# State space stage: rows of B and C spread a turn ahead, output projection in two halves

## The reference

```python
xz = x @ Win + bin                      # x is layernormed
xs, z = jnp.split(xz, 2, axis=-1)       # 256 inner channels each
xs = silu(xs)
xp = xs @ Wx + bx                       # dp (8), Bs (16), Cs (16)
delta = softplus(dp @ Wdt + bdt)
A = -jnp.exp(A_log)                     # 256 channels x 16 states
# for each token t, from h = 0:
h = exp(delta_t[:, None] * A) * h + (delta_t * xs_t)[:, None] * B_t[None, :]
hidden_t = h @ C_t
y = (hidden + xs * Dp) * silu(z)
x = x + y @ Wout + bout
```

## Time and profile before

| | |
|---|---|
| time, median of 3 runs | 6864.2 us (6859.29 to 6873.38) |
| the profiled execution | 6861.8 us, its span 6859.7 us |
| state space stage within it | about 1980 to 2684 us |
| busy over the whole span | PE 6081.4 us (89%), DVE 4362.3 (64%), ACT 3526.7 (51%), POOL 2191.8 (32%) |
| granted TensorE clock | mean 0.94 of full speed |

### The profile page before, as it was taken

One profiled execution on the slowest core, in us unless ns is written; L12 is line 12 of the kernel. 1 busy time (PEld: TensorE's weight loads), 2 busy tenths in 40 slices (PEclk: granted clock), 3 DMA queues, 4 the chain that ended last, 5 costly groups with the idle time before them and its releaser, 6 DMA issues. The chain is left out here.

```text
span 6859.7 us, 128543 instructions
## 1 busy us (share of the span) xinstructions
PE 6081.4 (89%) x50945; PEld 3477.3 (51%) x50945; DVE 4362.3 (64%) x7548; ACT 3526.7 (51%) x5768; POOL 2191.8 (32%) x1461
## 2 busy tenths in 40 slices
PE   7999987999877777998658999999999999999998
PEld 4666664444432223676434555555555555555554
DVE  3444443444348886333447888888888888888885
ACT  3434433666434443443425666666666666666664
POOL 0000000222214443000005555555555555555553
PEclk9999987999968888999769999999999999999999
DMA  1000000222200000000001111111111111111111
GB/s 52 1 1 1 1 1 13 50 50 49 61 8 0 0 1 0 1 0 0 0 22 35 32 41 41 32 38 42 35 37 43 36 34 45 36 32 46 39 37 26
DMA packets 183558, 174.97 MB, mean 26 GB/s; under 512 B 24021, under 2 KB 174070, under 8 KB 182774
## 3 DMA queue, kind: packets, MB, share of 16 engines
q1 hardware_dynamic: 182998, 167.18, 10.2%
HBM read 30.79 MB, written 2.10 MB: 5 GB/s over the span
## 5 line engine op out<-in xcount | busy, mean ns | idle before, releaser
L2367 POOL TENSOR_TENSOR local_ssum<-local_sq 128x512 f32<-128x512 f32 x384 | 696.3, 1813 | 2298.0 <-ACT local_sq L2155 2297.8
L2375 POOL TENSOR_TENSOR local_rot<-local_rot,local_inv_all 128x512 f32<-128x512 f32 x768 | 964.3, 1287 | 92.8 <-DMA local_inv_all<-local_inv 92.5
L1976 PE MATMUL banks<-local_y,local_Wqkv 128*128 128x512 f32 x1536 | 824.5, 619 | 63.9 <-ACT local_sq L2155 61.0
L861 POOL TENSOR_TENSOR cosine_summed<-cosine_probs 128x512 f32<-128x512 f32 x128 | 172.6, 1349 | 1678.6 <-ACT cosine_probs L750 1678.5
L2177 ACT ACTIVATE local_probs<-local_probs,local_npeak 128x1152 f32<-128x1152 f32 x384 | 482.7, 1257 | 355.2 <-DVE local_probs L2281 355.2
L2281 DVE TENSOR_TENSOR local_probs<-banks,band 128x576 f32<-128x576 f32 x768 | 546.2, 753 | 184.2 <-PE banks L2011 178.9
L2261 DVE TENSOR_TENSOR local_rot<-banks,local_rotary_scaled 128x512 f32<-128x512 f32 x768 | 525.6, 684 | 193.5 <-PE banks L1976 188.2
L2155 ACT ACTIVATE local_sq<-banks 128x512 f32<-128x512 f32 x768 | 459.4, 598 | 253.8 <-DVE local_sin L2262 244.1
L2268 DVE TENSOR_TENSOR local_rot<-local_rot,local_sin 128x1024 f32<-128x1024 f32 x384 | 512.3, 1334 | 41.2 <-DVE local_sin L2262 1.4
L2171 ACT COPY local_v<-banks 128x512 f32<-128x512 f32 x384 | 224.8, 586 | 595.0 <-PE banks L1989 594.5
L2011 PEld LDWEIGHTS banks<-local_rot 32*128 32x128 f32 x12288 | 415.5, 185 | 225.1 <-issue 202.4
(11 more groups left out here) (401 smaller groups left out, 10884.5 us busy)
## 6 DMA issues: line engine op xcount, KB each, us to landing
local_inv_all<-local_inv SPq DMA_DIRECT2D x768, 128.0 KB, 2.7
cosine_inv_all<-cosine_inv SPq DMA_DIRECT2D x256, 128.0 KB, 2.7
local_Wqkv<-in_L_ffn_Wqkv_quads SPq DMA_DIRECT2D x36, 256.0 KB, 2.8
local_Wo<-in_L_ffn_Wo_quads SPq DMA_DIRECT2D x6, 512.0 KB, 4.1
experts_w_W<-in_L_ffn_W SPq DMA_DIRECT2D x1, 2048.0 KB
out<-x SPq DMA_DIRECT2D x8, 256.0 KB, 2.3
local_W<-in_L_ffn_W SPq DMA_DIRECT2D x12, 170.5 KB, 2.4
cosine_w_Wqkv<-in_L_attn_w_kv SPq DMA_DIRECT2D x1, 1024.0 KB
```

What stands on the lines that cost most here:

```text
L1976: pe.matmul(seqs(banks[:, QK_BANK, :]), Wqkv[:, at:at + P], y_group(g), start=True, stop=True).then_inc(qk_projected, 1)
L2367: pool.tensor_tensor(ssum[:, n % 2, m, :], sq[:, 0, :], sq[:, 1, :], ALU.add).then_inc(square_summed, 1)
L2375: pool.tensor_tensor(a, a, twice(inv_all[:, n % 2, m, of_seq(s)]), ALU.mult).then_inc(united, 1)
```

## The change

At the head of its turn k TensorE spreads the rows of turn k+1, where it spread those of turn k. The output projection of a group is done in two halves of two tiles, one in turn 3 and one in turn 4 of the next group, each with a count of the semaphore out_ready; the addition to x moves from turn 4 to turn 5, and LAST grows by one. The two waits for out_ready count double.

```diff
-    GATE, WAY_OUT, ADD_OUT = 2, 3, 4
+    GATE, WAY_OUT, ADD_OUT = 2, 3, 5
@@ TensorE
-                def project_out(g):
+                def project_out(g, half):
                     pe.wait_ge(gated, CH * (g + 1))
-                    for t in range(GT):
+                    for t in range(half * GT // 2, (half + 1) * GT // 2):
@@ TensorE's order
                 for k in range(FIRST, LAST + 1):
-                    if scan_at(k) is not None:
-                        spread_rows(k)
+                    if scan_at(k + 1) is not None:
+                        spread_rows(k + 1)
                     if scan_at(k - 2) is not None:
                         gather(k - 2)
-                    if (g := finish_at(k, WAY_OUT)) is not None:
-                        project_out(g)
+                    for half in range(2):
+                        if (g := finish_at(k, WAY_OUT + half)) is not None:
+                            project_out(g, half)
@@ ScalarE, silu
-                        act.wait_ge(out_ready, m - 1)
+                        act.wait_ge(out_ready, 2 * (m - 1))
@@ VectorE, add_out
-                    dve.wait_ge(out_ready, g + 1)
+                    dve.wait_ge(out_ready, 2 * (g + 1))
```

## The result

| | before | changed |
|---|---|---|
| median | 6864.2 us, 7 runs (6859.29 to 6873.38) | 6890.85 us, 7 runs (6886.89 to 6895.18) |
| ratio | | 1.0037, 95% interval [1.0027, 1.0047] |
| profiled execution, span | 6861.8, 6859.7 | 6889.6, 6887.5 |
| first to last VectorE work of the stage | 1984.4 to 2681.2: 696.8 us | 1990.2 to 2712.3: 722.1 us |

The change makes the kernel 0.37% slower. The stage itself is 25.3 us longer. What lies ahead of it took 5.8 us more in this execution and what lies behind 3.3 less; those stages are the same code in both.

What follows compares the result with a forecast made beforehand. VectorE was taken to bound the state space stage, with 51.1 us of B waits to win at most. Order +11.5 and clock +10.5 and +8.4 gave +30.4, so 6894.6 us; range 6868 to 6925.

Steps and rivals of the forecast that it cites:

- group 7: Last group, which makes no next one: loses its 4.1 us of B waits, gets add_out's 1.5: -2.6 us.
- forecast: order: Sum at full clock: +8.4 us for the six middle groups, +5.7 for group 0, -2.6 for group 7: +11.5.
- forecast: clock: TensorE's clock falls after new idling: +10.5 us from turn 6, +8.4 from turns 9 or 11.
- The prices and the walk to turn 6: Middle group, turns 0 to 6: B waits reappear at add_out (1.5) and turn 6's scan (5.8); gain 0.2 us.
- Group 0: No projection sets the pace: 6.6 us wait at turn 6's scan, 1.8 and 1.0 later; +5.7 us against before.
- Turns 7 to 12 at full clock: Middle group: VectorE waits 1.8 us in turn 8 (1.18 before) and 1.0 in turn 10, new; turn 11 covered.
- The clock in turn 6: TensorE idles 3.8 us, drops to 1.2 GHz and delays turn 7's lowering: 1.5 us in 7 groups, +10.5.
- The clock in turn 9 or 11: TensorE idles 2.4 us ahead of each turn; a slow one costs 2.4 us in half the groups: +8.4.
- The first: Rival: TensorE's clock holds at 2.4 GHz, leaving +11.5 us, 6875.7; chance 0.20.
- The second: Rival: TensorE's turns 7, 9 and 11 are not held by the drive; -8.1 us, 6856; chance 0.07.
- The third: Rival: VectorE's B waits go and nothing takes their place; -51.1 us, 6813; chance 0.05.
- The fourth: Rival: TensorE stays at 1.2 GHz through turns 6 to 11 in most groups; up to +74 us, middle 6925; chance 0.13.

Runs made afterwards that it cites:

- e10_fill_more: The changed kernel with extra matmuls whose results nobody reads, where TensorE idles in turns 6, 8 and 10; 6873.9 us, ratio 1.0012.
- e2_halves_only: The changed kernel with the rows spread in their own turn as before, so only projection halves and later addition remain; 6863.45 us, ratio 0.9993.
- e7_ahead_early: The changed kernel with rows spread a turn ahead only for turns 3, 4 and 5 of each group; 6865.9 us, ratio 1.0002.
- e5_decays_ahead: e4_bias_later with ScalarE's decays of turn 6 put ahead of the silu of turn 5; 6855.6 us, ratio 0.9985.
- e4_bias_later: The changed kernel with VectorE's bias steps a turn later, BIAS 9 for 8 and BIAS_C 11 for 10; 6866.2 us, ratio 1.0000.

## Why the prediction was right

Forecast 6894.6 us, measured 6890.85. The times from turn 0 of one group to turn 0 of the next (group 7: to the last add_out), read from the traces of the kernel before, the changed one and e10_fill_more, against the terms of the sum, in us over the kernel before:

| | forecast: order | forecast: clock | changed kernel | clock held (e10) |
|---|---|---|---|---|
| group 0 | +5.7 | +2.7 | +7.26 | +4.58 |
| groups 1 to 6, each | +1.4 | +2.7 | +3.36 | +1.55 |
| group 7 | -2.6 | 0 | -3.18 | -3.37 |
| sum | +11.5 | +18.9 | +24.2 | +10.5 |

So the sum was 6 us too high for the turns themselves. The medians differ by 26.7; what lies outside the turns, in code that is the same in both kernels, took 3.6 us more in the profiled pair. That the forecast came within 4 us of the median is in part luck. By its steps:

- **The prices and the walk to turn 6**: the scan of turn 6 was put at 36.32 and came at 36.26; add_out's wait was put at 1.5 and came at 1.24, the scan's at 5.8 and came at 5.87. That one chain of work sets this scan in both orders is shown by e2_halves_only and e7_ahead_early, where the waits move and the scan stays. The prediction called it TensorE's own; e5_decays_ahead shows that its last part, the silu with its table loads ahead of the decays, is ScalarE's, and that the scan moves when this is cut.
- **Group 0**: its wait ahead of the scan of turn 6 was put at 6.6 and came at 5.26. The 8.01 from the first widening matmul to the scan was read in a middle group, where ScalarE loads a table (1.28 us) only once the first product is there. In group 0 it had loaded it 4 us ahead of the widening, and the scan came 6.67 after the first product's start.
- **Turns 7 to 12 at full clock**: put at 1.8 and 1.0, measured 1.75 and 0.81 once the clock was held (e10_fill_more). The sum of +11.5 was +8.6 there by the medians, inside its interval, and +10.5 by the turns.
- **The clock in turn 6**: right in mechanism, too large in size. I took 1.5 us for each group; turn 8 waits 2.44 in place of 1.75, so 0.7. The term was mis-sized because TensorE would have waited for drive 7 anyway (done at 2321.3, while the slow collecting ended at 2322.0), and the clock was back for all of turn 7.
- **The clock in turn 9 or 11**: I took 2.4 us in half of the groups. It was 1.53 in turn 12, in all middle groups, and 1.67 more in turn 10 in group 0. The step at half clock that I added (0.86) ran at full clock again; only the collecting was slow, 3.27 from its start to the next matmul for 1.72. The frequency was a guess between two rows: 1.2 taken for each group, 1.5 measured. That this error and the one in turn 6 have opposite signs is luck.
- Together the clock is 6890.85 - 6873.9 = 17 us by the medians and 24.2 - 10.5 = 13.7 by the turns, 18.9 in the forecast.

**The rivals.** The first, a clock that holds, is what e10_fill_more makes by force, and it measured 6873.9 where 6875.7 stood. Dropping the clock, as the prediction read the sentence of the Trainium skill (TensorE: Matmul & The Clock Gate, Part 1), would have given that number for the changed kernel. The sentence itself speaks of the ramp's penalty as under 1% of a kernel's span and of not fitting a count of cold matmuls. The measurement agrees with the size, for the clock's part here is 17 us, 0.25% of the span. But it is more than half of what the change did, so it can't be dropped from this sum. The second needed TensorE's turn 7 not to be held by the drive; it was held, the lowering started 42.9 us after turn 0 (42.1 in the walk), and turn 8 waited 2.4 for it. The third, all B waits won, had the right first half, 51.1 to 0, and the wrong second. The fourth, a clock that stays low through turns 6 to 11, is out: it is at 1.00 from 2322 to 2342 in the group shown.

## What to carry to other kernels

Work put at the head of an in-order queue with a wait moves all that stands behind it: before such a move, list what follows on that engine and who takes it, and move the takers as well. A wait that sits on a chain through another engine only changes its place when the order around it changes; follow the chain from one fixed event to the next and see if that time shifts. And compare the waits that appear with those that go, line by line: here the waits of VectorE in the turns grew by 23 us, and the turns by 24.

## What was not expected of the hardware

How long TensorE idled just before did not tell whether its clock would fall. In the changed kernel's group shown above it idled 2.19 us ahead of turn 9 and the clock stayed up, 2.09 ahead of turn 11 and it fell. In the kernel before it is at 0.50 in turn 12 of the same group, where the three idle stretches ahead of it were 0.57, 0.61 and 0.56 us, and four collecting matmuls take 3.64. Nobody waits for them there. The changed kernel's turn 9, then the kernel before's turn 12:

```profile
2332.38 0.39 PE L1070 MATMUL banks<-mamba_parts,mamba_pick 96*128 96x512 bf16 x1 [2.19 <-DVE banks L1256]
...
2332.82 1.88 PE L1081 MATMUL banks<-mamba_seen,ident 128*128 128x512 f32 x4
```

```profile
2320.02 3.64 PE L1081 MATMUL banks<-mamba_seen,ident 128*128 128x512 f32 x4 [0.56 <-POOL mamba_seen L1184]
...
2320.00:2322.00 2.00, 1.98 (x3) 0.95 (x4) 1.97 (x3) 1.39 (x3) 0.76 (x1) 0.50 0.00 0
```

What decides it these runs do not show. The fall can be moved: with the idling of turns 6 and 10 filled it came in turn 9 (turn 10's wait 0.5 to 2.2 in six groups of seven), and with turn 8 filled too it was gone from turns 6 to 11. A few matmuls without use gained 9 to 17 us on the changed kernel, and 9 on e4_bias_later, by the medians.
